# Mamba scan kernel: four pairs of states read out on each of VectorE and GpSimd, with three result tiles each

## The chip, the cores and the metric

The kernel runs as one program on one core of a Trainium2 chip. The metric is the device time of one execution in microseconds (us). Before the change it is 5198.36 us, the median of 3 runs (5197.64 to 5199.72). The engines are called by their own names and, in rows, by the profile's: TensorE (PE; its weight loads are PEld), VectorE (DVE), ScalarE (ACT), GpSimd (POOL) and SyncE (SP).

## The reference, cut to what matters

Two layers run one after the other on x, 64 sequences of 128 steps with 512 features in float32. Layer 0 is a conditioned Mamba block, layer 1 an attention block with a softmax over features. The change touches layer 0 alone. Its core, with DI = 1024 channels and N = 16 states per channel:

```python
xz = einsum('bsd,ed->bse', xn, in_proj_w);  x_in, z = split(xz, 2)
u  = silu(conv over 4 steps of x_in + conv_b)
dt_r, B, C = split(einsum('bsd,ed->bse', u, x_proj_w), [64, 80])
dt = softplus(einsum('bsr,dr->bsd', dt_r, dt_proj_w) + dt_proj_b)
def step(h, inp):                         # h is [b, DI, N]
    dA = exp(dt_t[:, :, None] * A)
    h  = h * dA + (dt_t * u_t)[:, :, None] * B_t[:, None, :]
    y  = einsum('bdn,bn->bd', h, C_t)     # the readout: times C, summed over the 16 states
    return h, y
y = (y + u * D_param) * silu(z);  out = x + gate * (y @ out_proj_w.T)
```

## The kernel before, in words

**Tiling.** A group is two sequences (GT = 256 columns), so there are 32 groups. In a group the 1024 channels are cut into four quarters (j = 0 to 3) of 256 channels, laid out as 128 partitions by 2. A quarter has 16 states, and one state of one quarter is a unit: 64 units a group, numbered q = 0 to 63. Two neighbouring states are a pair: 8 pairs a quarter, 32 a group, p = q // 2. In this text "unit 64" is unit 0 of the next group, "pair 32" its first pair.

**A unit's way.** ScalarE writes the decay exp(dt*A) of the unit into one of four slots of the tile dA, in PSUM (`decay`, L397). GpSimd multiplies du = dt*u with the rows of B for a whole pair and writes one of four dbu tiles (`scale_b`, L636). VectorE runs the recurrence along the 256 columns of 2 channel blocks in one instruction (L603). Then the pair is read out, that is, multiplied with C, in one of two ways:
- A D pair: the scans write in place into dA, and VectorE itself multiplies the pair with C into one of C_RING = 4 tiles hC (`readout` in the VectorE block, L537). It waits for its own scans first.
- A G pair: the scans write into one of two tiles hS, and GpSimd multiplies in place (`readout` in the GpSimd block, L647).

In both cases TensorE adds the pair into the PSUM tile Y with 8 matmuls of 128x128 against the identity (`accumulate`, L278). After the last pair of a quarter VectorE multiplies Y with the gate silu(z) (`gate_y`, L547), TensorE transposes it (L311), and ScalarE copies it out (L459). TensorE begins the next quarter's Y with the skip term (L300).

**Which pair goes where.** `KINDS = "GDGDDGDD"`: pairs 0, 2 and 5 of each quarter are G, the other five D. `D_PAIRS`, `G_PAIRS`, `ND` and `NGP` follow from it.

**What sets the order.** Every engine has its instructions in an order that is written out by hand, as functions of the unit q. `D_ACC` and `G_ACC` say at which unit (counted from the start of the quarter) TensorE adds a D or G pair; where both name the same unit, the D pair comes first. `G_LAG = 3` puts GpSimd's readout of pair p behind its product for pair p+3. `SIDE` holds the projections, the convolution and the rest of the work for the neighbouring groups ("Z" is the projection of z, L319; "CV" the convolution, which VectorE ends with L566; "DT" the step size, L571 and L574; "O" the output projection, L561). `YZ_AT` puts the four `gate_y` on VectorE behind units 18, 34, 50 and 66.

**What an engine waits for.** VectorE's scan of the first unit of a G pair waits until TensorE has added the G pair that had the same hS tile before (`yP_done`), its readout of a D pair the same for hC (`yD_done`). GpSimd's product p waits for the scan of pair p-4, whose dbu tile it takes. ScalarE's decay waits for its slot of dA (`bank_freed`): with a D pair until the readout, with a G pair until the scan.

**The loop.** `over_groups` (L202) writes groups 0 and 29 to 31 out straight and runs groups 1 to 28 in a hardware loop of 14 turns with two groups each. Between groups 2 and 3, 4 and 5 and so on an engine jumps back (13 times); group 1 is entered and group 29 reached at the loop's two ends. SyncE holds the loads of the rows of B and C (`bc`) for the next group back until the last reader of the old ones is through.

## Time and profile before

| | |
|---|---|
| runs | 5198.36 us median, 5197.64 to 5199.72 |
| the profiled execution | 5198.98 us, of which 5197.2 us are its span |
| busy share of the span | PE 88%, DVE 84%, ACT 60%, POOL 70%, PEld 63% |
| scans, L603 | x2048, about 1210 ns each |
| VectorE's readouts, L537 | x640, 1225 ns each |
| GpSimd's products, L636 | x1024, 2360 ns each |
| GpSimd's readouts, L647 | x384, 2358 ns each |

The units run from 127.6 us to 3916.3 us of the span; behind that comes layer 1, which the change does not touch. A timeline row gives the start, the time from there to the end of the last instruction merged into the row, engine, line, operation, tiles and count; in brackets stands how long the engine was idle before the row and what ended that. Instructions of one engine overlap a little at their ends, so the pace is read from start to start. A row of a window gives the stretch and its length, then for PE, PEld, DVE, ACT and POOL the busy time and the number of instructions, then TensorE's granted clock as a share of full speed, the DMA share and GB/s.

### The profile page before, as it was taken

How to read it: one execution, taken by the hardware profiler on the slowest of the kernel's cores; microseconds unless marked ns; L12 is line 12 of the kernel's file. 1: busy time of each engine (PE TensorE's matmuls, PEld its weight loads, DVE VectorE, ACT ScalarE, POOL GpSimd, SP SyncE). 2: the span in 40 equal slices, each digit the busy share in tenths (PEclk: the TensorE clock that was granted, in tenths of full speed). 3: DMA queues.
4: the chain of work that ended last, by engine and by line, in shares of the span. 5: the costliest groups of instructions: out<-in, count | busy, mean ns of one | idle time of the engine just before them, and what ended most of it. 6: DMA issues, size and time to landing. Idle time of an engine off the chain costs nothing. (4 is left out here: it accounts for less than half of the span.)

```text
span 5197.2 us, 75668 instructions
## 1 busy us (share of the span) xinstructions
PE 4553.3 (88%) x21856; PEld 3248.9 (63%) x21856; DVE 4353.0 (84%) x5203; ACT 3100.8 (60%) x7493; POOL 3659.4 (70%) x1733
## 2 busy tenths in 40 slices
PE   7888988888888988888888889898876999999997
PEld 4666666666666666666666666666654656565654
DVE  2999999999999999999999999999994656566664
ACT  2777767676776767676777667677762333333332
POOL 0888989888888889888888888899992222222222
PEclk8999999999999999999999999999987999999999
DMA  5111111111111111111112111111112111111111
GB/s 185 42 50 56 50 52 50 50 58 58 63 61 50 50 50 56 50 52 50 50 58 66 59 58 50 50 56 50 48 49 71 40 50 42 45 47 39 52 39 43
DMA packets 117994, 284.78 MB, mean 55 GB/s; under 512 B 15905, under 2 KB 21281, under 8 KB 117090
## 3 DMA queue, kind: packets, MB, share of 16 engines
q1 hardware_dynamic: 117602, 280.13, 16.2%
q8 instruction: 175, 2.87, 0.2%
q14 instruction: 217, 1.78, 0.1%
HBM read 245.35 MB, written 34.73 MB: 54 GB/s over the span
## 5 line engine op out<-in xcount | busy, mean ns | idle before, releaser
L636 POOL TENSOR_TENSOR dbu<-du,bc 128x1024 f32<-128x1024 f32 x1024 | 2395.5, 2360 | 216.4 <-DVE du L574 114.8
L397 ACT ACTIVATE dA<-dt,c_A 128x256 f32<-128x256 f32 x4096 | 1757.8, 466 | 696.4 <-DVE hC L537 640.5
L603 DVE TENSOR_TENSOR_SCAN dA<-dA,dbu 128x512 f32<-128x512 f32 x1280 | 1525.2, 1215 | 50.7 <-ACT dA L397 43.9
L647 POOL TENSOR_TENSOR hS<-hS,bc 128x1024 f32<-128x1024 f32 x384 | 905.7, 2358 | 313.6 <-DVE hS L603 309.1
L603 DVE TENSOR_TENSOR_SCAN hS<-dA,dbu 128x512 f32<-128x512 f32 x768 | 899.4, 1206 | 42.3 <-POOL dbu L636 27.8
L278 PE MATMUL Y<-c_ident,hC 128*128 128x128 f32 x5120 | 732.6, 290 | 209.2 <-DVE hC L537 206.8
L278 PEld LDWEIGHTS Y<-c_ident,hC 128*128 128x128 f32 x5120 | 620.8, 149 | 450.4 <-DVE hC L537 357.4
L537 DVE TENSOR_TENSOR hC<-dA,bc 128x1024 f32<-128x1024 f32 x640 | 783.7, 1225 | 64.7 <-DVE dA L603 6.5
L319 PE MATMUL side<-c_in_w,xnF 128*128 128x512 f32 x1024 | 559.7, 680 | 162.6 <-DVE u L566 115.9
L343 PE MATMUL side<-xin,c_conv_w 128*128 128x256 f32 x2048 | 491.5, 380 | 0.0
L336 PE MATMUL side<-xnF,c_in_w 128*128 128x256 f32 x2048 | 476.3, 381 | 10.9 <-ACT xnF L409 8.9
L324 PE MATMUL side<-c_out_w,yzF 128*128 128x512 f32 x1024 | 483.2, 595 | 0.8 <-ACT yzF L459 0.8
L278 PE MATMUL Y<-c_ident,hS 128*128 128x128 f32 x3072 | 426.4, 285 | 0.0
L343 PEld LDWEIGHTS side<-xin,c_conv_w 128*128 128x128 f32 x2048 | 376.5, 190 | 74.3 <-issue 28.7
L336 PEld LDWEIGHTS side<-xnF,c_in_w 128*128 128x128 f32 x2048 | 380.8, 191 | 61.0 <-ACT xnF L409 11.5
L319 PEld LDWEIGHTS side<-c_in_w,xnF 128*128 128x128 f32 x1024 | 202.7, 215 | 340.9 <-issue 215.5
L278 PEld LDWEIGHTS Y<-c_ident,hS 128*128 128x128 f32 x3072 | 378.2, 149 | 19.6 <-issue 16.4
L1076 POOL TENSOR_TENSOR p_k_e<-p_k_e,p_ksum 128x512 f32<-128x512 f32 x64 | 71.1, 1132 | 385.8 <-DVE p_ksum L1010 385.8
L930 ACT ACTIVATE p_q<-p_q 128x512 f32<-128x512 f32 x64 | 40.3, 629 | 440.2 <-POOL p_q L1080 440.2
L1080 POOL TENSOR_TENSOR p_q<-p_q,p_qmax 128x512 f32<-128x512 f32 x64 | 67.0, 1047 | 334.4 <-DVE p_qmax L1034 334.4
L300 PEld LDWEIGHTS Y<-c_skip_w,u 128*128 128x128 f32 x1024 | 147.1, 219 | 189.5 <-ACT yzF L459 155.3
L300 PE MATMUL Y<-c_skip_w,u 128*128 128x128 f32 x1024 | 168.1, 315 | 104.6 <-ACT yzF L459 104.6
(124 smaller groups left out, 5960.6 us busy)
## 6 DMA issues: line engine op xcount, KB each, us to landing
bc<-b_scratch SPq DMA_DIRECT2D x256, 512.0 KB, 4.0
x_in<-in_x SPq DMA_DIRECT2D x32, 512.0 KB, 5.0
gb<-gate_scratch SPq DMA_DIRECT2D x64, 256.0 KB, 4.0
xres<-in_x SPq DMA_DIRECT2D x64, 256.0 KB, 3.1
x_scratch<-xres SPq DMA_DIRECT2D x64, 256.0 KB, 2.0
p_x_in<-x_scratch SPq DMA_DIRECT2D x32, 512.0 KB, 4.0
p_xr<-x_scratch SPq DMA_DIRECT2D x32, 512.0 KB, 4.1
out<-p_xr SPq DMA_DIRECT2D x32, 512.0 KB, 3.1
```

Of the source, the lines that this page charges most:

```text
L278: last = pe.matmul(Y[:, b, k * P:(k + 1) * P], src[:, n, k, b * P:(b + 1) * P], C["ident"][:, :], start=False, stop=False, is_transpose=Tr ...
L300: last = pe.matmul(Y[:, b, k * P:(k + 1) * P], u[par][:, 2 * j + k, b * P:(b + 1) * P], W["skip"][:, 2 * j + k, :], start=(b == 0 and k == ...
L319: last = pe.matmul(out[:, :], xnF[par][:, part, b * P:(b + 1) * P], W["in"][:, part, DI + hf * D:DI + (hf + 1) * D], start=(part == 0), st ...
L324: last = pe.matmul(out[:, :], yzF[part // 2][par if part < 4 else 0][:, part % 2, j, :], W["out"][:, part, :], start=(part == 0), stop=(pa ...
L336: last = pe.matmul(out[:, half * GT:(half + 1) * GT], W["in"][:, k, e * P:(e + 1) * P], xnF[par][:, k, :], start=(k == 0), stop=(k == KD - 1))
L343: last = pe.matmul(out[:, half * GT:(half + 1) * GT].rearrange("p (b t) -> p b t", b=GB), W["conv"][:, e, t, :], xin[j % 2][:, half, :, t: ...
L397: last = act.activation(dA[:, q % A_RING, e, :], dt[j % 2][:, e, :], ACT.Exp, scale=C["A"][:, 2 * j + e, n:n + 1])
L537: dve.tensor_tensor(hC[i % C_RING][:, :, :, :], dA[:, k:k + 2, :, :], bc[:, 1, n:n + 2, :].unsqueeze(2).broadcast_to([P, 2, 2, GT]), ALU.m ...
L603: dve.tensor_tensor_scan(out.rearrange("p e t -> p (e t)"), dA[:, q % A_RING, :, :].rearrange("p e t -> p (e t)"), dbu[(q // 2) % B_RING][ ...
L636: gps.tensor_tensor(dbu[p % B_RING][:, :, :, :], du[j % 2][:, :, :].unsqueeze(1).broadcast_to([P, 2, 2, GT]), bc[:, 0, n:n + 2, :].unsquee ...
L647: gps.tensor_tensor(h, h, bc[:, 1, n:n + 2, :].unsqueeze(2).broadcast_to([P, 2, 2, GT]), ALU.mult).then_inc(hcP_done, 1)
L1076: gps.tensor_tensor(blk, blk, r, ALU.mult).then_inc(s["es_done"], 1)
```

## The change

`KINDS` becomes `"GGDGDGDD"`: pairs 0, 1, 3 and 5 of each quarter are G, and 2, 4, 6 and 7 are D. hC has three tiles in place of four, hS three in place of two. 16 pairs of each kind in a group are not a multiple of three, so the count of the addition that has to be over before a tile is written again comes from the new function `slot_free(i, ring, n)`: for the first three pairs of a group it takes the last pair of the group before that had the same tile. For i = 0 that is number 15 of 0 to 15, and the result is 0: all 16 of the group before.

```diff
+def slot_free(i, ring, n):
+    if i >= ring:
+        return i - ring + 1
+    return max(k for k in range(n) if k % ring == i) + 1 - n
-KINDS = "GDGDDGDD"
+KINDS = "GGDGDGDD"
-D_ACC = [6, 10, 11, 15, 17]
-G_ACC = [7, 12, 17]
+D_ACC = [8, 11, 15, 17]
+G_ACC = [7, 10, 14, 17]
 G_LAG = 3
-C_RING = 4
+C_RING = 3
+S_RING = 3
-    hS = [sb(f"hS{i}", [P, 2, 2, GT]) for i in range(2)]
+    hS = [sb(f"hS{i}", [P, 2, 2, GT]) for i in range(S_RING)]
@@ gpsimd_pair (TensorE)
-            accumulate(hS[i % 2]).then_inc(yP_done, 1)
+            accumulate(hS[i % S_RING]).then_inc(yP_done, 1)
@@ readout (VectorE)
-            wait(dve, yD_done, g * 4 * ND + (i - C_RING + 1))
+            wait(dve, yD_done, g * 4 * ND + slot_free(i, C_RING, 4 * ND))
@@ body (VectorE), the scan of a G pair
-                            wait(dve, yP_done, g * 4 * NGP + (i - 1))
-                        out = hS[i % 2][:, half, :, :]
+                            wait(dve, yP_done, g * 4 * NGP + slot_free(i, S_RING, 4 * NGP))
+                        out = hS[i % S_RING][:, half, :, :]
@@ readout (GpSimd)
-            h = hS[i % 2][:, :, :, :]
+            h = hS[i % S_RING][:, :, :, :]
```

The order of the instructions moves at three places that the prediction speaks of. The new lines stand 10 lines further down: L603 becomes L613, L537 L547, L566 L576, L278 L288, L636 L646, L647 L657, L319 L329.

VectorE where group 1 begins, before: `hC` and `hS` carry the tile's number, and the scan is called SCALAR_TENSOR_TENSOR here.

```order
L603 SCALAR_TENSOR_TENSOR hS1<-dA,dbu1 128x512 [waits dbu_ready,dA_ready]
...
L537 TENSOR_TENSOR hC3<-dA,bc 128x1024 [waits yD_done,scan_done]
L206 UNCONDITIONAL_BRANCH
...
L603 SCALAR_TENSOR_TENSOR hS0<-dA,dbu0 128x512 [waits yP_done]
...
L603 SCALAR_TENSOR_TENSOR hS1<-dA,dbu2 128x512 [waits yP_done,dbu_ready]
```

And the same place after.

```order
L613 SCALAR_TENSOR_TENSOR hS0<-dA,dbu1 128x512 [waits yP_done,dbu_ready,dA_ready]
...
L547 TENSOR_TENSOR hC0<-dA,bc 128x1024 [waits yD_done,scan_done]
L216 UNCONDITIONAL_BRANCH
...
L613 SCALAR_TENSOR_TENSOR hS0<-dA,dbu0 128x512 [waits yP_done]
...
L613 SCALAR_TENSOR_TENSOR hS1<-dA,dbu1 128x512 [waits yP_done]
```

Before, the last G pair of a group had tile hS1 and the first of the next one hS0. Now both have hS0, and the scan of unit 64 waits for the addition of the G pair 29.

TensorE at the same place, before: the two additions in front of the loop and the two behind its head, with the Z projection (L319) between them.

```order
L278 MATMUL Y<-c_ident,hS0 128x128 [waits hcP_done]
L278 MATMUL Y<-c_ident,hS0 128x128 x7
...
L278 MATMUL Y<-c_ident,hC2 128x128 [waits hcD_done]
L278 MATMUL Y<-c_ident,hC2 128x128 x7
L206 UNCONDITIONAL_BRANCH
...
L319 MATMUL side0<-c_in_w,xnF1 128x512 [waits xin_done]
L319 MATMUL side0<-c_in_w,xnF1 128x512
...
L278 MATMUL Y<-c_ident,hC3 128x128 [waits hcD_done]
L278 MATMUL Y<-c_ident,hC3 128x128 x7
...
L278 MATMUL Y<-c_ident,hS1 128x128 [waits hcP_done]
```

And after.

```order
L288 MATMUL Y<-c_ident,hS2 128x128 [waits hcP_done]
L288 MATMUL Y<-c_ident,hS2 128x128 x7
L288 MATMUL Y<-c_ident,hC2 128x128 [waits hcD_done]
L288 MATMUL Y<-c_ident,hC2 128x128 x7
L216 UNCONDITIONAL_BRANCH
...
L329 MATMUL side0<-c_in_w,xnF1 128x512 [waits xin_done]
L329 MATMUL side0<-c_in_w,xnF1 128x512
...
L288 MATMUL Y<-c_ident,hC0 128x128 [waits hcD_done]
L288 MATMUL Y<-c_ident,hC0 128x128 x7
L288 MATMUL Y<-c_ident,hS0 128x128 [waits hcP_done]
```

Behind the head nothing moved: two matmuls of Z, the D pair 31, then the G pair 29. The G pair in front of the head is now pair 27 (added at unit 62) and no longer pair 26 (unit 60).

GpSimd in the first quarter of group 1, before: products (dbu) and readouts (hS).

```order
L636 TENSOR_TENSOR dbu3<-du0,bc 128x1024
...
L647 TENSOR_TENSOR hS0<-hS0,bc 128x1024
L636 TENSOR_TENSOR dbu0<-du0,bc 128x1024
...
L636 TENSOR_TENSOR dbu1<-du0,bc 128x1024
...
L647 TENSOR_TENSOR hS1<-hS1,bc 128x1024
L636 TENSOR_TENSOR dbu2<-du0,bc 128x1024
...
L636 TENSOR_TENSOR dbu3<-du0,bc 128x1024
```

And after.

```order
L646 TENSOR_TENSOR dbu3<-du0,bc 128x1024
...
L657 TENSOR_TENSOR hS0<-hS0,bc 128x1024
L646 TENSOR_TENSOR dbu0<-du0,bc 128x1024
...
L657 TENSOR_TENSOR hS1<-hS1,bc 128x1024
L646 TENSOR_TENSOR dbu1<-du0,bc 128x1024
...
L646 TENSOR_TENSOR dbu2<-du0,bc 128x1024
...
L657 TENSOR_TENSOR hS2<-hS2,bc 128x1024
L646 TENSOR_TENSOR dbu3<-du0,bc 128x1024
```

Between product 3 and product 7 stand three readouts where two stood; one product alone is between the readouts of pairs 0 and 1.

## Rows read from the trace of the kernel before

**Rows 1.** The page: busy time of each engine; VectorE's busy tenths in 40 slices.

```profile
PE 4553.3 (88%) x21856; PEld 3248.9 (63%) x21856; DVE 4353.0 (84%) x5203; ACT 3100.8 (60%) x7493; POOL 3659.4 (70%) x1733
...
DVE  2999999999999999999999999999994656566664
```

**Rows 2.** Windows, groups 16, 17, 29 to 31: length, busy PE, PEld, DVE, ACT, POOL.

```profile
2030.80:2150.06 119.26, 101.55 (x535) 76.17 (x534) 112.52 (x115) 85.57 (x200) 107.33 (x48) 0.96 0.18 59
2150.06:2269.83 119.77, 107.81 (x539) 79.78 (x539) 112.70 (x114) 82.25 (x192) 102.65 (x45) 0.93 0.14 50
3581.00:3696.10 115.10, 102.74 (x538) 76.50 (x537) 112.40 (x115) 83.62 (x196) 104.88 (x47) 0.96 0.15 52
3696.10:3809.00 112.90, 96.38 (x481) 71.66 (x480) 111.01 (x111) 76.12 (x175) 104.81 (x47) 0.91 0.15 52
3809.00:3916.50 107.50, 77.18 (x378) 55.73 (x376) 105.25 (x100) 65.73 (x152) 97.74 (x44) 0.85 0.08 25
```

**Rows 3.** The page's groups: xcount, busy us, mean ns, idle before, its releaser.

```profile
L636 POOL TENSOR_TENSOR dbu<-du,bc 128x1024 f32<-128x1024 f32 x1024 | 2395.5, 2360 | 216.4 <-DVE du L574 114.8
...
L647 POOL TENSOR_TENSOR hS<-hS,bc 128x1024 f32<-128x1024 f32 x384 | 905.7, 2358 | 313.6 <-DVE hS L603 309.1
...
L537 DVE TENSOR_TENSOR hC<-dA,bc 128x1024 f32<-128x1024 f32 x640 | 783.7, 1225 | 64.7 <-DVE dA L603 6.5
```

**Rows 4.** Timeline of VectorE: a D pair, then a G pair, of group 15.

```profile
2017.86 2.33 DVE L603 TENSOR_TENSOR_SCAN dA<-dA,dbu 128x512 f32<-128x512 f32 x2
2020.31 1.22 DVE L537 TENSOR_TENSOR hC<-dA,bc 128x1024 f32<-128x1024 f32 x1
2021.45 2.33 DVE L603 TENSOR_TENSOR_SCAN hS<-dA,dbu 128x512 f32<-128x512 f32 x2
2023.70 2.32 DVE L603 TENSOR_TENSOR_SCAN dA<-dA,dbu 128x512 f32<-128x512 f32 x2
```

**Rows 5.** Timeline of VectorE: group 16 begins with the scan at 2030.80.

```profile
2029.65 1.22 DVE L537 TENSOR_TENSOR hC<-dA,bc 128x1024 f32<-128x1024 f32 x1
2030.80 1.21 DVE L603 TENSOR_TENSOR_SCAN hS<-dA,dbu 128x512 f32<-128x512 f32 x1
...
2034.94 0.68 DVE L547 TENSOR_TENSOR yz<-Y,zs 128x512 f32<-128x512 f32 x1
```

**Rows 6.** Timeline of TensorE at the same place.

```profile
2028.49 3.35 PE L319 MATMUL side<-c_in_w,xnF 128*128 128x512 f32 x4
2031.67 1.04 PE L278 MATMUL Y<-c_ident,hC 128*128 128x128 f32 x8
2032.55 1.04 PE L278 MATMUL Y<-c_ident,hS 128*128 128x128 f32 x8
2033.42 1.88 PE L319 MATMUL side<-c_in_w,xnF 128*128 128x512 f32 x4
```

**Rows 7.** Timeline of TensorE: last addition before the gate of group 15's third quarter.

```profile
2004.96 1.91 PE L278 MATMUL Y<-c_ident,hS 128*128 128x128 f32 x8
```

**Rows 8.** Timeline of VectorE: that gate.

```profile
2007.10 0.69 DVE L547 TENSOR_TENSOR yz<-Y,zs 128x512 f32<-128x512 f32 x1 [0.16 <-PE Y L278]
```

**Rows 9.** Timeline of VectorE behind the jump back, where group 17 begins.

```profile
2150.06 1.22 DVE L603 TENSOR_TENSOR_SCAN hS<-dA,dbu 128x512 f32<-128x512 f32 x1 [2.61 <-POOL dbu L636]
2154.10 0.88 DVE L566 SCALAR_TENSOR_TENSOR u<-side,c_cb,tmp 128x256 f32<-128x256 f32 x2 [2.82 <-issue]
...
2157.14 0.68 DVE L547 TENSOR_TENSOR yz<-Y,zs 128x512 f32<-128x512 f32 x1
```

**Rows 10.** Timeline of TensorE behind the jump back.

```profile
2149.72 3.77 PE L319 MATMUL side<-c_in_w,xnF 128*128 128x512 f32 x4 [3.95 <-issue]
...
2154.66 1.04 PE L278 MATMUL Y<-c_ident,hS 128*128 128x128 f32 x8
```

**Rows 11.** Timeline of GpSimd at the start of group 16.

```profile
2026.17 7.00 POOL L636 TENSOR_TENSOR dbu<-du,bc 128x1024 f32<-128x1024 f32 x3
2033.99 2.35 POOL L647 TENSOR_TENSOR hS<-hS,bc 128x1024 f32<-128x1024 f32 x1 [0.82 <-DVE hS L603]
```

## Prediction

> **What bounds the kernel now.** I read the busy shares first. VectorE and TensorE stand near 84 and 88% of the span, but VectorE's slices show 9 tenths in every slice of the Mamba layer and 4 to 6 behind it [rows 1]. The windows say it group by group: of the 119.26 us of group 16 VectorE is busy 112.52, TensorE 101.55, GpSimd 107.33, ScalarE 85.57 [rows 2]. What VectorE lacks to the full length in such a group is mostly the jump of the loop and the short gap between a pair's last scan and its readout. So VectorE sets the pace, and GpSimd follows at about 90%: it comes to a readout and waits for the scan that it reads (0.82 us), with the products of the next three pairs already made [rows 11]; 309 of the 314 us that it idles before its readouts end with a scan [rows 3]. The reader is to see two engines, one bound and one with a reserve of some 10%, and a change that takes work from the first and gives the second twice as much.
>
> **The gain on VectorE.** A D pair holds VectorE from 2017.86 to 2021.45, 3.59 us: two scans, the gap to the readout, the readout. The G pair behind it takes 2.25 (2021.45 to 2023.70) [rows 4]. The next D pair, 28 to 30 alike, reads 3.5 to 3.6 in the same way. I take 1.35 us for a pair that goes from D to G. There are 4 in a group and 128 in all: 128 x 1.35 = 172.8 us. Bounds: 1.23 us (the bare readout) to 1.37, so 157 to 175 us.
>
> **The new wait.** The order shows that the first G pair of a group now takes the tile of the last one of the group before (hS0 and hS0, before hS1 and hS0). For it `slot_free` gives 0, so VectorE's scan of unit 64 waits until TensorE has made all 16 additions of G pairs, the last of them pair 29. TensorE makes that one behind the D pair 31 in the same unit, and pair 31 is read out by VectorE directly before unit 64. So VectorE finishes its readout, waits until TensorE has done two times eight matmuls, and only then scans. Nothing but this one wait is worth a price: for the other pairs the tile is three G pairs old, and TensorE's addition of it stands 3 or more units ahead (pair 5 of a quarter, unit 10, takes the tile of pair 0, added at unit 7; the others take tiles from the quarter before). VectorE's readouts go through hC in the same way; the first in a group waits for the addition of pair 31, which is over when unit 64 may start. Behind the waiting scan stand CV's two instructions for u, the scans of units 65 and 66 and the gate; ScalarE's decays and GpSimd's readout of pair 32 hang on those scans.
>
> The price, where the group follows straight on: the scan of unit 64 started at 2030.80 [rows 5]. The D addition began at 2031.67, since TensorE was still in the Z projection, and the G addition ended at 2032.55 + 1.04 = 2033.59 [rows 6]. How long VectorE needs from such an end shows where it waited for one: the addition ended at 2004.96 + 1.91 = 2006.87 [rows 7], the gate started at 2007.10 [rows 8], so 0.23 us. 2033.59 + 0.23 - 2030.80 = 3.0 us. Nothing pays it back: the gate at 2034.94 followed its scan without a wait [rows 5], so it had no idle time to lose.
>
> The price at the loop's jump: there VectorE started unit 64 at 2150.06 and then stood 2.82 us more before u, the gate came at 2157.14 [rows 9]. TensorE is later still there (3.95 us in "issue" before Z); the G addition ends at 2154.66 + 1.04 = 2155.70 [rows 10]. Unit 64 would start at 2155.93. From unit 64 to the gate VectorE needs 2034.94 - 2030.80 = 4.14 us of work [rows 5], so the gate comes at 2160.07: 2.9 us later than before. That counts the 2.82 us as hidden in the wait, because what is fetched late would be fetched while the scan waits. If it is not hidden, it is 5.7 us.
>
> 31 boundaries at 3.0 us are 93 us. From below: TensorE's first two Z matmuls (four records) took 3.35 us, the next four records of the same kind 1.88 [rows 6]. Had the first been as fast, the D addition would start with the readout's end at 2030.87 and the G addition end 1.92 later, and the wait were 2.2 us, 68 in all. From above 13 x 5.7 + 18 x 3.0 = 128.
>
> **What GpSimd has to carry.** One product or readout takes it 2.33 us from start to start (7.00 us for three [rows 11]; 2360 and 2358 ns by themselves [rows 3]). I count 4 x 2.32 = 9.3 us more per group. Two groups, one turn of the loop, last 119.26 + 119.77 = 239.0 us, GpSimd being busy 107.33 + 102.65 = 210.0 [rows 2]; it idles 29.0. After: GpSimd 210.0 + 18.6 = 228.6; VectorE 239.0 - 10.8 + 3.0 + 2.9 = 234.1. GpSimd keeps 5.5 us a turn, but these lie at the jump. In the group without the jump VectorE needs 119.26 - 2.61 (the jump [rows 9]) - 5.4 + 3.0 = 114.2, and GpSimd the mean of 105.0 and 9.3, 114.3. They are even, and each wobbles by a product against the other. I charge 1 us a turn, 14 us, for scans that find their product late; the bounds are 0, from the three products of lead [rows 11], and 3 us a turn, 42, a product more in each turn.
>
> In the last three groups VectorE has less work beside the scans, and GpSimd becomes the bound: 104.88 + 9.3 = 114.2 against 115.10 - 5.4 + 3.0 = 112.7; 104.81 + 9.3 = 114.1 against 112.90 - 5.4 + 3.0 = 110.5; 97.74 + 9.3 = 107.0 against 107.50 - 5.4 = 102.1 [rows 2]. That is 1.5 + 3.6 + 4.9 = 10.0, less a part of the lead that GpSimd brings along: 6 us (0 to 10).
>
> TensorE has the same 32 additions a group as before and 14 us or more idle in each of the two windows [rows 2]; one addition more or less before another costs nothing while it waits for VectorE. ScalarE's slot of dA comes free a readout sooner in one pair of a quarter more than before, and as many D pairs as before are followed by a G pair (three); I take 0. The loads of C wait for the readouts as before, with whole microseconds to spare; 0.
>
> **The sum**, against the profiled execution, 5198.98 us (span 5197.2, 1.8 around it; 0.6 over the median of the runs): 5199.0 - 172.8 + 93 + 14 + 6 = 5139 us.
>
> **The rivals.**
> - *No wait to speak of at the boundary.* It would be so if the addition of pair 29 were long done. For it: the scan waits for pair 29 alone, GpSimd has read it out before TensorE gets there. Against: the order puts TensorE's pair 31 in front of it. Then a turn is GpSimd's, 228.6, VectorE's 228.2 below it, and the last groups cost 4.5 + 6.6 + 4.9 = 16 less 5. 5199.0 - 172.8 + 14 x 1.5 + 11 = 5058 us.
> - *The jump's second gap is not hidden.* VectorE stands its 2.82 us before u also after the longer wait, 13 times: 5139 + 37 = 5176 us. For it: the gap came right after the first scan, with no waiting engine named [rows 9]. Against: the longer wait gives 5.9 us in which to fetch.
> - *GpSimd becomes the bound and the kernel slower than before.* The place is the first quarter's half where GpSimd reads out pairs 0 and 1 with one product between. If a readout, waiting for its scan at the head of GpSimd's queue, holds the products back, VectorE waits for those. It decides from the point where GpSimd still idles (239.0 - 228.6) / 2 = 5.2 us in a group. If 6 us a group of its idle time stay, a turn is 240.6 (+1.6, 14 turns: 22) and the last three groups 120.2, 120.1 and 113 (+5, +7, +5.5): 5199 + 40 = 5239 us. For it: most of its idle time ends with a scan [rows 3]. Against: that is so because it is ahead; the later it comes, the less it waits.
>
> The readout costs 1225 ns on VectorE and 2358 on GpSimd, 1.92 times as much [rows 3]. The Trainium skill, GPSIMD Engine Reference, section 4.1 (Engine selection), speaks against this change: elementwise products belong on VectorE, since GpSimd is about twice as slow with two inputs. The trace agrees in the ratio. By that rule without GpSimd's reserve the 128 moved readouts would lengthen the kernel by 128 x 2.32 = 297 us, to 5496 us; GpSimd's 29 idle us a turn [rows 2] speak against it, and I give it 1 in 100, beside the third rival.
>
> **How the numbers follow.** The forecast 0.70, its own range 5112 to 5165; no wait at the boundary 0.08; the second gap not hidden 0.14; GpSimd the bound, with the page's case, 0.08. A difference of 0.2%, 10 us, is about what a measurement of this kernel can tell from no change. The range is 5095 to 5185: from most of the gain with the low price of the wait (5199 - 175 + 68 + 0 + 0 = 5092) to the second rival with some more of GpSimd's lateness. It leaves out the first rival and the third. Faster by over 0.2% (below 5188) 0.88, within it 0.05, slower 0.07.
>
> **What would show it.** Right: a row of VectorE's scan in hS with about 3 us idle, ended by PE Y, 31 of them in some form, at group starts; VectorE's readouts x512 with 1225 ns; GpSimd's readouts x512, its idle time before them down from 314 us to a small part; the gate no longer waiting at group starts; a turn of the loop near 235 us. Wrong: scans that wait for GpSimd's products by more than some 40 us in total (the coupling), 2.8 us of "issue" before u that stay at the jumps (the second rival), or no idle time before the first scan of a group (the first). The forecast falls if a turn of the loop is under 231 us or over 238.

## The result and the profile after

The changed kernel takes 5052.86 us (median of 4 runs, 5050.48 to 5058.92) against 5198.44 us before; the ratio is 0.9721, 95% interval 0.9705 to 0.9738. It is faster, as forecast, but by 146 us and not by 60: the time lies under the stated range (5095 to 5185), and next to the first rival's 5058 us, whose mechanism did not occur. The profiled execution took 5058.92 us, its span is 5057.1; it is the slowest of the four runs, 6 us over their median.

The page of the changed kernel, first the busy times, then GpSimd's tenths; they answer to [rows 1].

```profile
PE 4449.8 (88%) x21856; PEld 3181.9 (63%) x21856; DVE 4197.5 (83%) x5075; ACT 3086.4 (61%) x7493; POOL 3938.8 (78%) x1861
...
POOL 0999999999999999999999999999981222222222
```

GpSimd now shows 9 tenths throughout the Mamba layer. The groups, xcount | busy us, mean ns | idle before and what ended it; compare [rows 3].

```profile
L646 POOL TENSOR_TENSOR dbu<-du,bc 128x1024 f32<-128x1024 f32 x1024 | 2411.6, 2389 | 114.7 <-DVE du L584 114.7
...
L613 DVE TENSOR_TENSOR_SCAN hS<-dA,dbu 128x512 f32<-128x512 f32 x1024 | 1209.8, 1208 | 168.8 <-PE Y L288 114.8
L657 POOL TENSOR_TENSOR hS<-hS,bc 128x1024 f32<-128x1024 f32 x512 | 1223.8, 2390 | 22.8 <-DVE hS L613 22.8
...
L547 DVE TENSOR_TENSOR hC<-dA,bc 128x1024 f32<-128x1024 f32 x512 | 626.6, 1224 | 22.4 <-DVE dA L613 5.7
```

Three things are to be seen. The new wait is there: 114.8 us of VectorE's scans in hS end with PE Y, in 31 waits. GpSimd's idle time before its readouts fell from 313.6 to 22.8 us. And the idle time before VectorE's readouts fell from 64.7 to 22.4 us, more than 128 readouts fewer can explain.

The loop is read best in one stretch of 13 turns, from the first scan of group 3 to that of group 29: us, then busy time (instructions) of PE, PEld, DVE, ACT, POOL, then TensorE's granted clock. Before:

```profile
478.05:3580.97 3102.92, 2730.95 (x13939) 2032.76 (x13938) 2927.29 (x2965) 2179.85 (x5092) 2727.32 (x1195) 0.94 0.16 54
```

After, with the last three groups, and then groups 16 and 17 by themselves, as in [rows 2]:

```profile
469.41:3438.93 2969.52, 2629.33 (x13937) 1966.30 (x13936) 2798.03 (x2861) 2169.26 (x5096) 2950.96 (x1298) 0.98 0.17 56
3438.93:3775.01 336.08, 275.89 (x1376) 202.45 (x1374) 315.08 (x310) 223.29 (x519) 336.08 (x149) 0.90 0.14 46
...
1953.69:2070.19 116.50, 102.17 (x537) 76.13 (x536) 107.71 (x111) 83.49 (x196) 116.50 (x53) 0.97 0.19 62
2070.19:2182.38 112.19, 100.45 (x537) 75.06 (x536) 107.52 (x110) 83.43 (x196) 110.94 (x49) 0.98 0.16 51
```

A turn went from 3102.92 / 13 = 238.7 us to 228.4; I had forecast 234.1. GpSimd is busy in all of group 16 and in 110.94 of the 112.19 us of group 17. In the last three groups it is busy all 336.08 us and so is the bound, as forecast; they got 1.7 us longer than before (334.35 from the first scan of group 29 to the last scan of group 31).

**The boundary.** VectorE at the start of group 16 in the changed kernel, against [rows 5]:

```profile
1948.03 2.33 DVE L613 TENSOR_TENSOR_SCAN dA<-dA,dbu 128x512 f32<-128x512 f32 x2
1950.40 1.22 DVE L547 TENSOR_TENSOR hC<-dA,bc 128x1024 f32<-128x1024 f32 x1
1953.68 1.22 DVE L613 TENSOR_TENSOR_SCAN hS<-dA,dbu 128x512 f32<-128x512 f32 x1 [2.06 <-PE Y L288]
...
1957.84 0.66 DVE L557 TENSOR_TENSOR yz<-Y,zs 128x512 f32<-128x512 f32 x1
```

TensorE at the same place, against [rows 6]:

```profile
1948.17 1.09 PE L288 MATMUL Y<-c_ident,hC 128*128 128x128 f32 x8 [0.80 <-DVE hC L547]
1949.10 1.88 PE L329 MATMUL side<-c_in_w,xnF 128*128 128x512 f32 x4
1951.68 1.09 PE L288 MATMUL Y<-c_ident,hC 128*128 128x128 f32 x8 [0.70 <-DVE hC L547]
1952.61 1.04 PE L288 MATMUL Y<-c_ident,hS 128*128 128x128 f32 x8
```

The wait has the place and the cause of the forecast, but is 2.06 us long. Z's four records take 1.88 us and not 3.35, so TensorE stands ready when the readout ends, and the D addition starts 0.06 us behind it, where it was 0.80 late before. The scan starts 0.03 us after the G addition's end (1952.61 + 1.04 = 1953.65), where I had taken 0.23. Before, TensorE had idled 2.04 us in front of the addition of pair 30 and of Z:

```profile
2027.34 1.36 PE L278 MATMUL Y<-c_ident,hC 128*128 128x128 f32 x8 [2.04 <-DVE hC L537]
```

The granted clock (third number from the end) of TensorE during the Z matmuls, before and after:

```profile
2028.50:2031.60 3.10, 3.10 (x5) 1.23 (x5) 2.98 (x3) 1.75 (x5) 3.10 (x3) 0.53 0.64 211
```

```profile
1949.10:1951.60 2.50, 1.88 (x6) 0.58 (x4) 2.46 (x3) 1.66 (x4) 2.50 (x3) 1.00 0.16 57
```

For nearly all of Z it was at the lower level, 1.2 GHz, before, and it is at 2.4 GHz now, behind 0.80 us of idle time.

**The jump.** VectorE and TensorE where group 17 begins, against [rows 9, 10]:

```profile
2063.01 1.22 DVE L547 TENSOR_TENSOR hC<-dA,bc 128x1024 f32<-128x1024 f32 x1
2070.19 1.22 DVE L613 TENSOR_TENSOR_SCAN hS<-dA,dbu 128x512 f32<-128x512 f32 x1 [5.96 <-PE Y L288]
2071.33 0.85 DVE L576 SCALAR_TENSOR_TENSOR u<-side,c_cb,tmp 128x256 f32<-128x256 f32 x2
...
2074.34 0.67 DVE L557 TENSOR_TENSOR yz<-Y,zs 128x512 f32<-128x512 f32 x1
```

```profile
2064.74 3.10 PE L329 MATMUL side<-c_in_w,xnF 128*128 128x512 f32 x4 [3.01 <-issue]
2067.63 1.65 PE L288 MATMUL Y<-c_ident,hC 128*128 128x128 f32 x8
2069.11 1.04 PE L288 MATMUL Y<-c_ident,hS 128*128 128x128 f32 x8
```

The gap of 2.82 us before u is gone into the wait: u follows the scan at once, which the second rival had denied. From the end of the last readout to the gate 10.1 us pass, 9.3 before (means over the 13 jumps; here 2074.34 - 2064.23).

### The profile page after: what moved, and what is told of

The parts are those of the page before. It is cut to its first block and busy times, and to the rows that moved or that the text cites. A ratio compares the mean times of both kernels' runs of the same rounds, so it can differ in the third digit from the quotient of the medians.

```text
span 5057.1 us, 75222 instructions
## 1 busy us (share of the span) xinstructions
PE 4449.8 (88%) x21856; PEld 3181.9 (63%) x21856; DVE 4197.5 (83%) x5075; ACT 3086.4 (61%) x7493; POOL 3938.8 (78%) x1861
## 5 line engine op out<-in xcount | busy, mean ns | idle before, releaser
L646 POOL TENSOR_TENSOR dbu<-du,bc 128x1024 f32<-128x1024 f32 x1024 | 2411.6, 2389 | 114.7 <-DVE du L584 114.7
L613 DVE TENSOR_TENSOR_SCAN hS<-dA,dbu 128x512 f32<-128x512 f32 x1024 | 1209.8, 1208 | 168.8 <-PE Y L288 114.8
L657 POOL TENSOR_TENSOR hS<-hS,bc 128x1024 f32<-128x1024 f32 x512 | 1223.8, 2390 | 22.8 <-DVE hS L613 22.8
L613 DVE TENSOR_TENSOR_SCAN dA<-dA,dbu 128x512 f32<-128x512 f32 x1024 | 1205.0, 1211 | 25.4 <-ACT dA L407 18.4
L288 PEld LDWEIGHTS Y<-c_ident,hC 128*128 128x128 f32 x4096 | 484.5, 144 | 284.8 <-DVE hC L547 188.0
L288 PE MATMUL Y<-c_ident,hC 128*128 128x128 f32 x4096 | 555.9, 280 | 121.5 <-DVE hC L547 117.9
L547 DVE TENSOR_TENSOR hC<-dA,bc 128x1024 f32<-128x1024 f32 x512 | 626.6, 1224 | 22.4 <-DVE dA L613 5.7
L329 PE MATMUL side<-c_in_w,xnF 128*128 128x512 f32 x1024 | 537.3, 651 | 119.7 <-DVE u L576 80.0
L288 PE MATMUL Y<-c_ident,hS 128*128 128x128 f32 x4096 | 542.3, 276 | 15.9 <-POOL hS L657 15.9
L288 PEld LDWEIGHTS Y<-c_ident,hS 128*128 128x128 f32 x4096 | 480.9, 143 | 99.3 <-issue 65.4
L329 PEld LDWEIGHTS side<-c_in_w,xnF 128*128 128x128 f32 x1024 | 188.4, 202 | 269.6 <-issue 180.0
L334 PEld LDWEIGHTS side<-c_out_w,yzF 128*128 128x128 f32 x1024 | 179.4, 192 | 131.9 <-issue 129.9
L792 PE MATMUL pair<-p_wo,p_hF 128*128 128x512 f32 x512 | 232.7, 598 | 9.9 <-POOL p_hF L1080 9.9
```

Of the source, the lines that this page charges most:

```text
L288: last = pe.matmul(Y[:, b, k * P:(k + 1) * P], src[:, n, k, b * P:(b + 1) * P], C["ident"][:, :], start=False, stop=False, is_transpose=Tr ...
L329: last = pe.matmul(out[:, :], xnF[par][:, part, b * P:(b + 1) * P], W["in"][:, part, DI + hf * D:DI + (hf + 1) * D], start=(part == 0), st ...
L334: last = pe.matmul(out[:, :], yzF[part // 2][par if part < 4 else 0][:, part % 2, j, :], W["out"][:, part, :], start=(part == 0), stop=(pa ...
L547: dve.tensor_tensor(hC[i % C_RING][:, :, :, :], dA[:, k:k + 2, :, :], bc[:, 1, n:n + 2, :].unsqueeze(2).broadcast_to([P, 2, 2, GT]), ALU.m ...
L613: dve.tensor_tensor_scan(out.rearrange("p e t -> p (e t)"), dA[:, q % A_RING, :, :].rearrange("p e t -> p (e t)"), dbu[(q // 2) % B_RING][ ...
L646: gps.tensor_tensor(dbu[p % B_RING][:, :, :, :], du[j % 2][:, :, :].unsqueeze(1).broadcast_to([P, 2, 2, GT]), bc[:, 0, n:n + 2, :].unsquee ...
```

## The experiments

Where a result is set against "the changed kernel", that one has 228.4 us a turn (its profiled stretch of 13 turns) and 5053 us (its median). Each diff is against the changed kernel. The runs stand in three series; the kernel before took 5194.1, 5198.1 and 5198.2 us in them (5198.4 with the changed kernel). In the first series (four and two tiles, each engine's readout lighter, the count of 20) the kernel before is 4 us faster, so a difference in us to the changed kernel is up to 4 us off there, and the ratios are the better measure. The changed kernel's own four runs spread over 8.4 us.

### Four and two tiles: does the wait cost what it lasts?

```diff
-C_RING = 3
-S_RING = 3
+C_RING = 2
+S_RING = 4
```

> The changed kernel with four tiles hS and two hC (16 is a multiple of both), so the first scan of a group no longer waits for the last G pair. Theory V (VectorE sets the pace of the changed kernel and the wait at the group's start is paid in full): a turn of the loop, 228.4 us now, loses 2.1 us at the straight boundary and about 0.7 at the jump, where the gap of 2.8 us before u comes back; 14 turns and five straight boundaries give some 50 us, about 5005 us. Theory E (VectorE and GpSimd are even): GpSimd's 96 products and readouts of 2.32 us and four additions of 1.24 make 227.4 us a turn, so at most 1 us a turn and a few in the straight groups: 0 to 20 us, 5033 to 5053 us. The 31 waits for PE Y of 114.8 us vanish under both.

Measured: 5039.9 us, ratio 0.9703 (0.9690 to 0.9717). The wait for PE Y before the first scan is gone. What VectorE idles before scans in hS and before its readouts:

```profile
L613 DVE TENSOR_TENSOR_SCAN hS<-dA,dbu 128x512 f32<-128x512 f32 x1024 | 1211.7, 1209 | 96.6 <-ACT dA L407 60.6 <-POOL dbu L646 23.1 <-issue 7.8
...
L547 DVE TENSOR_TENSOR hC<-dA,bc 128x1024 f32<-128x1024 f32 x512 | 626.6, 1224 | 50.2 <-DVE dA L613 6.2
```

And its 13 turns:

```profile
459.59:3420.41 2960.82, 2641.85 (x13940) 1979.58 (x13940) 2803.56 (x2860) 2168.44 (x5093) 2955.19 (x1300) 0.97 0.17 57
```

115 us of waits went and 13 us of time (9 us by the ratios, whose intervals overlap): a turn is 227.8 us, GpSimd busy in 2955.19 of 2960.82, as theory E said. But this is no clean test of it. The readouts' idle time rose from 22.4 to 50.2 us, which the edit did not aim at (the count of 20 below shows where such gaps come from), and so 28 us of the 115 came back on VectorE by themselves. The test without this flaw is the G pair added first, at the end.

### Each engine's readout made lighter, then both

```diff
@@ readout (GpSimd): gpsimd_light; readout (VectorE): vector_light; both_light has both
+            w = 1 if m == NGP - 1 else 2
-            gps.tensor_tensor(h, h, bc[:, 1, n:n + 2, :] ...
+            gps.tensor_tensor(h[:, 0:w, :, :], h[:, 0:w, :, :], bc[:, 1, n:n + w, :] ...
+            w = 1 if m == ND - 1 else 2
-            dve.tensor_tensor(hC[i % C_RING][:, :, :, :], dA[:, k:k + 2, :, :],
+            dve.tensor_tensor(hC[i % C_RING][:, 0:w, :, :], dA[:, k:k + w, :, :],
```

> The changed kernel with GpSimd's readout of pair 5 of each quarter done for the first of its two states only (the output loses the factor C of the other state). 128 readouts get 1.16 us shorter, 148 us of GpSimd. Theory G (GpSimd alone sets the pace): 5053 - 140 = about 4915 us. Theory E (even): only VectorE's waits for products go, 10 to 20 us, 5035 to 5043. Theory V (VectorE): 5053, no difference.

> The changed kernel with VectorE's readout of pair 7 of each quarter done for the first of its two states only (the second half of the tile hC keeps old values). 128 readouts get 0.53 us shorter, 68 us of VectorE. Theory V: 5053 - 65 = about 4988 us. Theory E: at most 1 us a turn, 5035 to 5050. Theory G: 5053.

> The changed kernel with both cuts at once: VectorE's readout of pair 7 and GpSimd's of pair 5 for one state only (the output is missing those factors of C). Alone the first moved the loop's turn from 228.4 us to 227.8 and the second to 228.3. Theory E (two engines each at the limit, VectorE near 228.3 and GpSimd near 227.4 a turn): together they give what neither gives alone, VectorE's 8 x 0.53 = 4.2 us a turn: 224.1 us a turn and, with the shorter last groups, about 4975 us. Rival X (a third thing, TensorE or ScalarE, holds the turn at 228): no less than 5030 us.

These kernels leave out the factor C of one state in a pair. Measured: GpSimd lighter 5037.8 us (ratio 0.9695, 0.9681 to 0.9710), VectorE lighter 5050.5 (0.9725, 0.9710 to 0.9740), both 4985.9 (0.9593, 0.9577 to 0.9609). The 13 turns and the last three groups, GpSimd lighter:

```profile
467.40:3435.07 2967.67, 2631.55 (x13937) 1968.62 (x13936) 2795.49 (x2860) 2169.49 (x5096) 2844.46 (x1300) 0.98 0.17 56
3435.07:3758.81 323.74, 269.10 (x1376) 197.27 (x1374) 312.96 (x310) 222.84 (x519) 319.95 (x147) 0.93 0.13 44
```

The 13 turns with VectorE lighter, and with both:

```profile
466.88:3428.76 2961.88, 2633.14 (x13937) 1965.52 (x13936) 2747.94 (x2861) 2170.96 (x5096) 2953.53 (x1300) 0.98 0.17 57
```

```profile
461.83:3386.58 2924.75, 2611.93 (x13937) 1962.20 (x13936) 2743.62 (x2860) 2170.76 (x5096) 2842.43 (x1300) 0.99 0.17 57
```

VectorE with 50 us less to do in the stretch gains 8 us of it, GpSimd with 107 us less gains 2; together they gain 45. The 8 and the 2 us are no more than the spread of the changed kernel's own runs, and by the ratios the lighter VectorE is not faster at all (0.9725 against 0.9721); the 45 us are clear of it. So both engines are at their limit in the loop, 228.3 us a turn for VectorE (the lighter GpSimd shows it) and 227.8 for GpSimd. Theory E had 224.1 us a turn and 4975 us for both cuts, 225.0 and 4986 were measured; rival X, a third engine holding 5030 us, is out. GpSimd's cut paid mostly in the last three groups, 12 us (336.1 to 323.7), where it is the bound. Neither engine "is the bottleneck"; a cut on one alone is worth 0.6 us a turn or less, a cut on both 3.4.

### Where VectorE's readout lost its gap

```diff
-            accumulate(hC[i % C_RING]).then_inc(yD_done, 1)
+            accumulate(hC[i % C_RING]).then_inc(yD_done, 5 if i == 4 * ND - 1 else 1)
@@ readout (VectorE)
-            wait(dve, yD_done, g * 4 * ND + slot_free(i, C_RING, 4 * ND))
+            free = slot_free(i, C_RING, 4 * ND)
+            wait(dve, yD_done, g * 20 + (free - 4 if i < C_RING and free < 0 else free))
@@ gate_y
-            wait(dve, yD_done, g * 4 * ND + ND * (j + 1))
+            wait(dve, yD_done, g * 20 + (20 if j == 3 else ND * (j + 1)))
```

> The changed kernel with yD_done counting 20 in a group (the last addition of a D pair adds 5), so that its thresholds are no longer multiples of the same 16 as those of yP_done; nothing else differs. In the trace of before 0.12 us lie between a pair's last scan and its readout in the loop, in that of after 0.035. Theory R (thresholds that share one register leave no register instruction between the two; this is part of the gain of the change): the gap goes back to 0.12 us, 16 x 0.09 = 1.4 us a group; with VectorE at the limit 20 to 45 us longer, 5073 to 5098 us, and 1.4 us a turn less if GpSimd sets the pace. Rival (the gap has to do with tiles or banks, not with registers): the gap stays at 0.035 us and the time at 5053.

Measured: 5083.4 us, ratio 0.9782 (0.9767 to 0.9797), 30 us over the changed kernel. VectorE at the end of its group 15, then the group of readouts:

```profile
1962.66 2.33 DVE L614 TENSOR_TENSOR_SCAN dA<-dA,dbu 128x512 f32<-128x512 f32 x2
1965.12 1.22 DVE L548 TENSOR_TENSOR hC<-dA,bc 128x1024 f32<-128x1024 f32 x1
```

```profile
L548 DVE TENSOR_TENSOR hC<-dA,bc 128x1024 f32<-128x1024 f32 x512 | 626.8, 1224 | 52.8 <-DVE dA L614 6.4
```

From scan to readout 1965.12 - 1962.66 = 2.46 us, in the changed kernel 1950.40 - 1948.03 = 2.37. Idle time before readouts is 52.8 us against 22.4. The order of VectorE's instructions shows the reason. Before, a register instruction that waits for the scan stands in front of most readouts in the loop; in the changed kernel the readout waits for both semaphores itself:

```order
L33 REGISTER_ALU [waits scan_done]
L537 TENSOR_TENSOR hC1<-dA,bc 128x1024 [waits yD_done]
```

```order
L547 TENSOR_TENSOR hC2<-dA,bc 128x1024 [waits yD_done,scan_done]
```

With 16 additions of each kind and three tiles of each, the thresholds for pair i of either kind are the same number, and the G pair's scan has put it into a register a little earlier. Counting 20, or four tiles against two, takes that away; two and two below keeps it. The traces agree readout by readout: before, 448 of the 640 readouts have more than 0.1 us in front, and a register instruction stands directly ahead of just these 448; with the count of 20 it is 364 of 512, again the same ones; in the changed kernel no readout has one, and 28 have more than 0.1 us in front. So the gap and its cause are shown.

What the gaps cost in time is not, although the kernel got longer by just their 30 us. The 13 turns with the count of 20:

```profile
470.08:3466.71 2996.63, 2629.89 (x13937) 1963.52 (x13936) 2793.02 (x2860) 2169.41 (x5096) 2952.07 (x1298) 0.98 0.17 56
```

Of these 27 us over the changed kernel 22 lie at the jumps: there VectorE takes 11.8 us from its last readout to the gate in place of 10.1, because TensorE idles 4.0 us in "issue" and not 3.1, and then runs Z more slowly (means of 13). Inside the groups the gaps before readouts grew by 28 us, but VectorE's other waits there, mostly for ScalarE and for GpSimd's products, shrank by 18 and its busy time by 5, so that only 5 us are left. Nothing here separates the two parts, and why TensorE starts later at the jump stays open.

### Two tiles, and the change's two halves alone

```diff
@@ ring22                     @@ kinds_only                 @@ rings_only
-C_RING = 3                   -C_RING = 3                   -KINDS = "GGDGDGDD"
-S_RING = 3                   -S_RING = 3                   -D_ACC = [8, 11, 15, 17]
+C_RING = 2                   +C_RING = 4                   -G_ACC = [7, 10, 14, 17]
+S_RING = 2                   +S_RING = 2                   +KINDS = "GDGDDGDD"
                                                            +D_ACC = [6, 10, 11, 15, 17]
                                                            +G_ACC = [7, 12, 17]
```

> The changed kernel with two tiles hS and two hC. 16 is a multiple of 2, so the first scan of a group waits for pair 27 and not for pair 29; and both kinds have the same depth again, so VectorE's readout finds its threshold in a register that the scan of a G pair has used before. Theory R (registers): the gap before the readout stays at 0.035 us, where four and two tiles had 0.12. Theory E (VectorE and GpSimd even): a turn of the loop cannot fall under GpSimd's 227.4 us, so the time is that of four and two tiles, 5040 us, within 5 us, although VectorE has some 5 us less to do in a turn. Theory V (VectorE sets the pace alone): 2 x 16 x 0.09 = 2.8 us a turn less than with four and two tiles, 5000 us. Rival T (two tiles hS are too few for two G pairs in a row): scans wait for PE Y at each quarter, over 1 us each, 5053 us or more.

> One part of the change alone: four pairs each (the new KINDS, D_ACC and G_ACC) with the tiles of before, two hS and four hC. The wait at the group's start is gone, and nearly all readouts have their threshold in a register. Theory E: as four and two tiles, 5035 to 5045 us, the tiles of the change being worth nothing or less than nothing. Rival (the third tile hS is what lets VectorE run): 5060 us or more, with scans waiting for PE Y within the quarters.

> The other part alone: five and three pairs as before, with three tiles hS and three hC. 12 is a multiple of 3, and 20 is not, but hC's first readout of a group waits for an addition long made. Theory: no wait appears and none goes, 5194 us within 8. Rival (part of the gain comes from the third tile hS): 5180 us or less.

Measured: two and two tiles 5257.2 us (ratio 1.0113, 1.0096 to 1.0130), the new kinds alone 5260.1 (1.0123, 1.0106 to 1.0139), the tiles alone 5198.6 (1.0003, 0.9993 to 1.0012). What ended VectorE's idle time before its scans, two and two tiles, then the new kinds alone:

```profile
  PE Y L288: 310.3, 177
```

```profile
  PE Y L288: 310.3, 176
```

And the 13 turns of the new kinds alone:

```profile
482.36:3628.46 3146.10, 2715.00 (x13937) 2008.64 (x13936) 2804.53 (x2861) 2169.50 (x5092) 2959.38 (x1300) 0.96 0.16 53
```

My theory E failed here. I had expected 5040 us for both, and they are slower than the kernel before. With two tiles hS the scans wait 177 times for an addition, 310 us; a turn is 242.0 us, and GpSimd is idle 14 us of it. The largest mean gaps inside the groups lie at units 22 (2.95 us), 6 (2.32), 54 and 38, each the first scan of a quarter's pair 3: pair 3 takes the tile of pair 0, whose addition TensorE has at unit 7, behind the point where VectorE wants it. So the third tile hS is what makes four G pairs pay, and by itself it is worth nothing: neither half of the change is of use without the other. Rival T and the rival of the new kinds alone were right. The registers' part came out as expected: with two and two tiles the gap stayed at 0.035 us in the loop.

### TensorE's clock in front of the wait

```diff
@@ add60: G_ACC               @@ slow60: body (VectorE), behind the scan of a unit
-G_ACC = [7, 10, 14, 17]      +                    if q == 60:
+G_ACC = [7, 10, 12, 17]      +                        dve.tensor_reduce(extra[:, :], bc[:, 1, 12:16, :], AX.XY, ALU.add)
```

> The changed kernel with TensorE's addition of the last but one G pair of a quarter at unit 12 in place of 14, where the kernel before had its own. In the trace of before TensorE idles 2.04 us before the addition of pair 30 and then runs Z's four matmul records at half the clock (2.56 us from the first start to the last), in that of after 0.80 us and 1.29. Theory C (that idle stretch lowers the clock, the Z projection gets slow, and the addition of pair 29 late; this is why the forecast took 3.0 us for the wait and 2.1 were measured): TensorE idles 1.5 us or more there, Z takes 2.56 again, and the wait at straight boundaries rises from 2.06 to about 2.9 us, up to 5 us longer in all where GpSimd has room for it. Rival (the clock there has to do with the whole kernel's load): idle time up, Z still 1.29, the wait still 2.06.

> The changed kernel with one more instruction on VectorE after the scan of unit 60: a sum over 1024 elements into a tile that nothing reads, about 1.1 us. It makes TensorE wait longer in front of the addition of pair 30, as before the change. Theory C (that idle stretch goes with the clock: 0.80 us before it and Z's four records take 1.29 us from first to last start, 2.04 us and they take 2.56, which makes the addition of pair 31 and with it the wait at the group's start late): TensorE's idle time there about 1.9 us, Z 2.56, and VectorE's wait at straight boundaries 2.7 to 2.9 us in place of 2.06. Rival: idle time 1.9, Z still 1.29, wait 2.06. The time itself rises by up to 32 x (1.1 + 0.8) = 61 us, 5110 us.

Measured: the addition moved to unit 60, 5051.0 us (0.9715, 0.9699 to 0.9731); the extra instruction, 5091.7 us (0.9799, 0.9783 to 0.9816). TensorE at the end of a group with the addition moved:

```profile
1949.26 1.09 PE L288 MATMUL Y<-c_ident,hC 128*128 128x128 f32 x8 [0.81 <-DVE hC L547]
1950.19 1.88 PE L329 MATMUL side<-c_in_w,xnF 128*128 128x512 f32 x4
```

TensorE idled 0.81 us and not the 1.5 or more of theory C. So this run did not make the idle stretch that it was to test, and tells only that the place of the addition was not its cause. The extra instruction did. TensorE, then VectorE, with the extra instruction:

```profile
1965.99 1.40 PE L289 MATMUL Y<-c_ident,hC 128*128 128x128 f32 x8 [1.93 <-DVE hC L548]
1967.18 3.31 PE L330 MATMUL side<-c_in_w,xnF 128*128 128x512 f32 x4
1970.33 1.04 PE L289 MATMUL Y<-c_ident,hC 128*128 128x128 f32 x8
```

```profile
1972.28 1.22 DVE L614 TENSOR_TENSOR_SCAN hS<-dA,dbu 128x512 f32<-128x512 f32 x1 [2.83 <-PE Y L289]
```

Theory C holds in 10 of the 13 straight boundaries: 1.19 us of work on VectorE gave TensorE 1.93 us of idle time in place of 0.80, Z took 3.31 us, and VectorE's wait grew from 2.06 to 2.83. In the other 3 the clock stayed up with the same 1.94 us of idle time, and there the wait stayed at 2.06. So it is the clock that makes the wait longer, and a stretch of this length mostly, not always, goes with the lower one. Why the changed kernel has the shorter stretch is argued, not shown: TensorE does the same work as before in a shorter group.

### The order of TensorE's additions at the boundary

```diff
@@ g_first                    @@ z_later: SIDE
-G_ACC = [7, 10, 14, 17]      -    ("Z", 0, 0, [0, 0, 2, 2]),
+G_ACC = [7, 10, 14, 16]      +    ("Z", 0, 0, [2, 2, 2, 2]),
```

> The changed kernel with TensorE's addition of the last G pair of a quarter at unit 16 in place of 17, so that pair 29 is added in front of Z and of pair 31. Theory W (the wait at the group's start is made of the sixteen matmuls behind VectorE's own last readout): it falls from 2.06 to 1.0 us or less at straight boundaries, what is left being GpSimd's readout of pair 29, which ended 0.1 us before VectorE's last readout of the group; at the jumps, where the addition would stand in front of Z, from 5.9 to 3 us or less. Theory E: GpSimd's 227.4 us a turn hold the gain under 1 us a turn, 5035 to 5053 us. Rival (the wait does not come from the order but from GpSimd): it stays at 2 us.

> The changed kernel with the first two parts of the first Z projection at unit 2 in place of 0, so that behind the loop's jump TensorE has the two additions first. Theory W: the wait for PE Y at the jumps falls by Z's three microseconds, from 5.9 to about 3 us, and stays near 2.06 at the straight boundaries, or rises to 2.9 where TensorE, idle for longer, runs the additions at half the clock. Theory E: in time at most 1 us a turn, 5035 to 5053 us. Rival (the jump's wait is the fetch of TensorE's code alone): still 5 us or more at the jumps.

Measured: the G pair first, 5035.0 us (0.9692, 0.9675 to 0.9708); Z later, 5049.4 us (0.9718, 0.9702 to 0.9735). TensorE with the G pair first: the additions of pair 30, then 29, then Z, then 31.

```profile
1938.83 1.09 PE L288 MATMUL Y<-c_ident,hC 128*128 128x128 f32 x8 [0.35 <-DVE hC L547]
1939.88 1.09 PE L288 MATMUL Y<-c_ident,hS 128*128 128x128 f32 x8
1940.81 1.88 PE L329 MATMUL side<-c_in_w,xnF 128*128 128x512 f32 x4
1942.53 1.04 PE L288 MATMUL Y<-c_ident,hC 128*128 128x128 f32 x8
```

The scan's wait falls to a mean of 0.63 us at the straight boundaries and 3.54 at the jumps. Theory W said 1.0 or less, and 3 or less at the jumps. The first mean covers ten boundaries with 0.43 us or less and three with 1.9 to 2.7, where Z again ran more slowly. With Z later TensorE idles longer and pays with its clock; the additions of pairs 31 and 29:

```profile
1944.12 1.97 PE L288 MATMUL Y<-c_ident,hC 128*128 128x128 f32 x8 [2.42 <-DVE hC L547]
1945.88 1.83 PE L288 MATMUL Y<-c_ident,hS 128*128 128x128 f32 x8
```

Sixteen matmuls took 3.6 us in place of 2.0, the wait rose to a mean of 3.17 at the straight boundaries and fell at the jumps from 5.9 to 5.1 only: 5 us or more was the rival's number. What ate the saving is not fetch alone: where group 17 begins TensorE idled 3.96 us in "issue" (3.01 in the changed kernel) and then ran the two additions in 3.7 us, at half the clock. In time Z later gives nothing (0.9718 against 0.9721).

The G pair first has the lowest median of the kernels that do all the work, 18 us under the changed one, with the kernels before within 0.2 us of each other in the two series; their intervals overlap a little (0.9675 to 0.9708, 0.9705 to 0.9738), and four and two tiles (0.9690 to 0.9717) cannot be told from it. Its readouts have the same 22.4 us in front as the changed kernel's, so it is the clean test of theory E: 51 of the 115 us of waits went, 18 us of time, and a turn is 227.7 us, of which GpSimd is busy 227.3.

## Why the prediction was wrong, point by point

The forecast was 5139 us, the profiled execution took 5059. Two terms of the sum failed: the price of the new wait, 93 us forecast and 50 measured, and the gain on VectorE, which took the other readouts as unchanged while the gaps before them shrank by 29 us.

- *VectorE sets the pace, GpSimd has 10% in reserve.* Right before. The change spends all of it, as worked out: GpSimd 228.6 us a turn forecast, 227.0 of 228.4 busy measured.
- *The gain on VectorE, 172.8 us.* The size of the moved readouts is right as far as the runs tell. What failed is the bound "1.23 to 1.37": the change also took something from the 512 readouts that stay. Their gap fell from a mean of 0.101 to 0.044 us, 29 us in all (64.7 - 22.4 idle, less 128 x 0.101). The count of 20 gave these gaps back, and with them 30 us of time, of which however most lay at the jumps; so the 29 us are VectorE's idle time, and how much of them reached the kernel's time is open. I had not looked at the register instructions that stand between wait and readout.
- *The new wait, 93 us.* The mechanism was right to the instruction, the term mis-sized. From the last readout's end to the gate VectorE took 4.06 us at straight boundaries and takes 6.23: 2.2 us and not 3.0. At the jumps it is 10.08 against 9.31: 0.8 us and not 2.9. 18 x 2.2 + 13 x 0.8 = 50 us. At the straight boundaries there are two causes: Z ran at the full clock, since TensorE no longer idled 2 us in front of it (the extra instruction shows what the clock does to the wait), and the reaction of 0.23 us, which belongs to the gate, was put on a scan that reacts in 0.04. At the jumps TensorE's addition of pair 29 starts 4.8 us behind the last readout in place of 6.9 (means of 13): the addition of pair 30 in front of the jump takes 1.1 us and not 1.8, Z takes 0.6 us less, and TensorE idles 3.05 us in "issue" and not 3.59. The last of these has no explanation here. My bound from below, 2.2 us, was that case, and I set it aside by taking TensorE's rows as they stood in a kernel whose pace the change itself alters.
- *The jump's second gap hidden.* Right: no idle time before u at the jumps.
- *GpSimd's lateness, 14 us, and the last groups, 6 us.* In the last groups GpSimd is the bound as said, but they cost more: 336.1 us with GpSimd busy throughout, where about 331 followed from the working. In the loop the two engines are even, and scans wait for products 17.3 us in total. Of the charge of 14 us I can show no more than that.
- *The sum.* 5139 - 43 (the wait) - 29 (the gap) = 5067, against the profiled 5059. The remaining 8 us are about what the gates' waits for TensorE fell by (13.3 to 3.8 us idle before L547, now L557), and also no more than the spread of the four runs; their cause is not shown. Nor is it shown that terms add up in a loop where two engines are even: where VectorE got faster by itself, most of it did not reach the time.
- *ScalarE, TensorE, the loads: nothing.* Right for VectorE: its scans waited 58.5 us for ScalarE's decays before and 54.0 after. TensorE has new idle time of its own, 48.9 us before the transposes of yz (3.3 before) and 49.0 before a projection that waits for zs (2.0 before). It had less in reserve than I wrote: the two windows leave 17.7 and 12.0 us idle, not 14 or more in each.
- *The rivals.* The first named the right time for the wrong reason: a lucky number. With its premise (no wait) the kernel took 5040 us, with most of the wait gone 5035. Its 5058 also has a slip: a turn of 228.6 in place of 228.2 us adds 14 x 0.4 and not 14 x 1.5, which gives 5043, near those two. The second did not occur: no idle time stands before u at the jumps. The third was wrong in its course: GpSimd coming later waited less.
- *The rule on engine selection.* The Trainium skill, GPSIMD Engine Reference, section 4.1 (Engine selection), has elementwise work with two inputs on VectorE, GpSimd being about twice as slow. The trace agrees in the ratio (2358 to 1225 ns), but the rule would have decided wrongly here: the kernel with one readout a quarter more on GpSimd takes 5053 us against 5198.
- *Not priced at all:* two tiles for four G pairs. The third tile was taken as given; without it the change costs 62 us.

## What to carry to other kernels

When two engines come out even in a forecast, price a cut on each and on both: the loop then takes the larger of two sums, and taking 51 us of a visible wait away was worth 18 us. Where the use of a ring of buffers is numbered anew in each period and its depth does not divide the count, the first uses of a period wait for the last ones of the period before, and it is to be checked what that wait costs; here it cost nothing for hC and 50 us for hS. The depth that a ring needs follows from where the consumer stands in its own order, here a tile more. The durations of an engine that another one paces are no constants: TensorE's Z took 3.35 us before the change and 1.88 after. And a time that comes out as expected does not show the expected cause: the count of 20 cost its 30 us mostly in another place.

## What the runs showed of the hardware

- A register instruction between a wait and the instruction costs about 0.09 us on VectorE: 2.46 against 2.37 us from a pair's first scan to its readout, 30 us of idle time over 512 readouts. A scan that waits for TensorE itself starts 0.03 to 0.04 us after the last matmul's modelled end in 28 of the 31 waits, 0.14 in the others; the gate of the kernel before, with register and semaphore instructions between, mostly 0.22 us.
- At the 13 straight boundaries TensorE ran Z at 2.4 GHz each time behind 0.80 us of idle time (the changed kernel) and behind 1.10 us (four and two tiles), and more slowly in 10 of 13 behind 1.94 us (the extra instruction) and in 12 of 13 behind 2.04 us (the kernel before). Z's four records take 1.88 us at 2.4 GHz and up to 3.35 otherwise.
- Behind the loop's jump TensorE stands 2.5 to 4.8 us in "issue" before its first matmul (before, after, count of 20, G pair first, Z later), and in the kernel before VectorE 2.6 us and then 2.8 us more one instruction later. In the changed kernel, where a wait of 5.96 us stands at the first instruction, the second gap is gone.
- GpSimd's products and VectorE's scans kept their pace beside each other: GpSimd 2.32 us from start to start before and after, though it is now busy 99% of the loop (2950.96 of 2969.52 us), and scans about 1210 ns each. GpSimd's mean duration by the rows rose from 2360 to 2389 ns all the same, so starts are the better measure.
